# Expert tiles with three buffers in place of two, two PSUM banks for each tile in flight, and a new order of turns, products and results

## What is computed

```python
h = layernorm(x) * (1 + ca) + sa
x = x + ga * mamba(h)                       # conv, selective scan over time, gate, projection
h = layernorm(x) * (1 + cb) + sb
probs = softmax(h @ router_w.T); top_w, top_idx = top_k(probs, 2)
g = einsum('th,eih->tei', h, gate_w)        # E = 8, I = 352, H = 128
u = einsum('th,eih->tei', h, up_w)
y = einsum('tei,ehi,te->th', silu(g) * u, down_w, one_hot_weights(top_w, top_idx))
x = x + gb * y
```

## Time and profile before

| | us |
|---|---|
| median of 3 runs (687.80 to 689.67) | 689.32 |
| the profiled execution | 686.06 |
| its span, first to last instruction | 684.3 |
| TensorE busy | 618.2 (90%) |
| VectorE busy | 552.9 (81%) |
| ScalarE busy | 532.9 (78%) |
| GpSimd busy | 507.5 (74%) |
| scan, up to the first expert tile's load | to about 498 |
| first turn of a tile to the last down product | 500.3 to 669 |
| combination and end | 669 to 684.3 |

### The profile page before, as it was taken

The page is one execution under the profiler, slowest core; times in us unless marked ns, Lnnn a source line. Parts: engine busy times, 40 slices in busy tenths (PEclk is TensorE's granted clock), DMA queues, the critical chain, the costliest instruction groups (busy, mean ns, idle before and its releaser), DMA issues.

```text
span 684.3 us, 14573 instructions
## 1 busy us (share of the span) xinstructions
PE 618.2 (90%) x4473; PEld 518.8 (76%) x4473; DVE 552.9 (81%) x1165; ACT 532.9 (78%) x996; POOL 507.5 (74%) x487
## 2 busy tenths in 40 slices
PE   8988789989989998998998998769789999999995
PEld 6447667867857766786786777658678899999994
DVE  4568797899899999989899999999975586555554
ACT  3689977979998997998999799797834756665650
POOL 5249889877899898899989989977946557644441
PEclk9999999999999999999999999999999999999998
DMA  7303334545634643344544445475612223222545
GB/s 242 125 2 95 95 95 129 157 110 177 208 108 126 172 127 106 117 126 122 158 106 108 107 131 160 118 192 131 176 34 58 65 65 86 82 65 65 154 148 196
DMA packets 65195, 82.93 MB, mean 121 GB/s; under 512 B 6960, under 2 KB 55152, under 8 KB 61024
## 3 DMA queue, kind: packets, MB, share of 16 engines
q1 hardware_dynamic: 59648, 70.78, 38.1%
q0 software_dynamic: 4320, 9.12, 4.0%
q10 hardware_dynamic: 1152, 2.10, 0.8%
HBM read 52.19 MB, written 29.78 MB: 120 GB/s over the span
## 4 chain that ended last, share of the span: by engine, by line
PE 35%; ACT 28%; DVE 14%; issue 11%; POOL 9%; DMA 1%; DVEq 0%; SPq 0%; ACTq 0%; POOLq 0%
PE psum L606 24%; ACT S L1071 10%; PE psum L610 10%; ACT dA L1079 10%; DVE ring L1466 7%; POOL ring L576 5%; POOL S L555 2%; POOL token_rows L477 1%; ACT xn L982 1%; ACT L1019 1%; ACT soft L1010 1%; DMA ring<-results 1%; ACT h2r L1044 1%; ACT soft L1019 1%; ACT soft L1012 1%
## 5 line engine op out<-in xcount | busy, mean ns | idle before, releaser
L576 POOL TENSOR_TENSOR ring<-ring,Cb 128x1024 f32<-128x1024 f32 x128 | 279.2, 2182 | 46.0 <-DVE ring L1466 45.4
L610 PEld LDWEIGHTS psum<-ident,S 128*128 128x128 f32 x1024 | 120.9, 144 | 111.7 <-issue 54.4
L610 PE MATMUL psum<-ident,S 128*128 128x128 f32 x1024 | 161.3, 282 | 41.9 <-POOL S L555 17.3
L1079 ACT ACTIVATE dA<-delta,A 128x512 f32<-128x512 f32 x256 | 178.3, 715 | 10.5 <-DVE ring L1466 10.3
L1071 ACT ACTIVATE S<-duT,BT 128x256 f32<-128x256 f32 x384 | 166.4, 500 | 22.3 <-issue 13.3
L610 PE MATMUL psum<-ident,ring 128*128 128x128 f32 x1088 | 161.3, 280 | 4.0 <-DMA ring<-results 3.7
L1466 DVE TENSOR_TENSOR_SCAN ring<-dA,state,psum 128x512 f32<-128x512 f32 x128 | 157.8, 1266 | 2.5 <-PE psum L610 1.9
L1466 DVE TENSOR_TENSOR_SCAN ring<-dA,psum 128x512 f32<-128x512 f32 x128 | 150.0, 1205 | 2.5 <-PE psum L610 2.2
L610 PEld LDWEIGHTS psum<-ident,ring 128*128 128x128 f32 x1088 | 131.2, 146 | 5.0 <-DMA ring<-results 4.2
L598 POOL DMA_INDIRECT results<-xn,result_at x71 | 68.8, 969 | 74.6 <-DVE xn L1583 64.9
L606 PE MATMUL psum<-uT,S 128*128 128x128 f32 x852 | 107.1, 275 | 1.0 <-DVE uT L1561 1.0
(11 more groups left out here) (218 smaller groups left out, 726.8 us busy)
## 6 DMA issues: line engine op xcount, KB each, us to landing
Cb<-c_rows SPq DMA_DIRECT2D x32, 1024.0 KB, 6.0
token_rows<-zeros SPq DMA_DIRECT2D x64, 272.0 KB, 7.1
uT<-token_rows SPq DMA_DIRECT2D x71, 68.0 KB
ring<-results SPq DMA_DIRECT2D x8, 512.0 KB, 4.9
xT<-in_xT SPq DMA_DIRECT2D x4, 512.0 KB, 5.0
out_T<-xT ACTq DMA_DIRECT2D x8, 256.0 KB, 2.3
stage<-in_xT SPq DMA_DIRECT2D x6, 256.0 KB, 7.1
gateup_w<-in_gate SPq DMA_DIRECT2D x1, 1408.0 KB, 8.3
```

Source lines behind the costliest of these rows:

```text
L576: nc.gpsimd.tensor_tensor(ring[:, k % RING, :, 0:BANK], ring[:, k % RING, :, 1:], Cb[:, group_ % 2, own, :].unsqueeze(1).to_broadcast([P, ...
L610: return nc.tensor.matmul(out, block_in, ident[at, at], is_transpose=True, start=start, stop=True, skip_group_check=True)
L1079: nc.scalar.activation(dA[:, (k * HALVES + a) % DA_SLOTS, :], delta[:, s % 2, a, :], ACT.Exp, scale=A[:, a, n:n + 1]).then_inc(da_ready, 1)
```

## The change

The slots of `xsT`, `both_w`, silu and `innerT` become three (DEEP = 3); silu and `innerT` move into the space of dA, so that `both_w` has S for itself. Each tile in flight now has two PSUM banks: the gate product and the turn share one (2, 3 or 6), and the up and the down product share the other (4, 5 or 1), at different columns. A step's order is new on each engine that computes: TensorE makes gate and up of tile k, turns tile k+2, and makes down of tile k-2; ScalarE makes silu of k ahead of the weights' copy for k+2; VectorE makes inner of k, copies the turn of k+2 and weights the result of k-2. Gate of tiles 0 to 2, up of tiles 0 and 1 and the first three turns stand between the last `add_state` calls of the scan.

```diff
-XS_SLOTS = 4
+XS_SLOTS, DEEP = 4, 3
...
         def PG(k):
-            return bank(2 + k % 2)
+            return bank((2, 3, 6)[k % DEEP])
+        def PX(k):
+            return PG(k if k else DEEP - 1)[:, NIN * P:BANK]
         def PU(k):
-            return bank((4, 1)[k % 2])
+            return bank((4, 5, 1)[k % DEEP])
         def PO(k):
-            return bank((5, 0)[k % 2])[:, 0:P]
+            return PU(k)[:, NIN * P:BANK]
...
+            def turn_row(k):
...
+                wait(pe, silu_ready, k - DEEP + 1)
+                turn(PX(k), xs[:, slot, 0:HID]).then_inc(xt_filled, 1)
...
-            def up_product(k, par):
-                wait(pe, inner_ready, k - 1)
+            def up_product(k):
+                wait(pe, o_read, k - DEEP + 1)
...
-            def tile(k, par, rnd):
...
+            def tile(k):
+                if k == 0:
+                    gate_product(2)
+                if k == 1:
+                    turn_row(3)
+                    down(0)
+                if 2 <= k < TILES:
+                    if k > 2:
+                        gate_product(k)
+                    up_product(k)
+                if 2 <= k < TILES - 2:
+                    turn_row(k + 2)
+                if k >= 3:
+                    down(k - 2)
...
-            gate_product(0, 0)
-            for k in range(STEPS - LAG, STEPS):
-                for a in range(HALVES):
-                    add_state(k, a)
-            up_product(0, 0)
+            gate_product(0)
+            turn_row(1)
+            for a in range(HALVES):
+                add_state(STEPS - 3, a)
+            up_product(0)
+            gate_product(1)
+            for a in range(HALVES):
+                add_state(STEPS - 2, a)
+            up_product(1)
+            turn_row(2)
+            for a in range(HALVES):
+                add_state(STEPS - 1, a)
...
+            def tile(k):
+                if k == 1:
+                    copy_weights(3)
+                if 2 <= k < TILES:
+                    activate(k)
+                if 2 <= k < TILES - 2:
+                    copy_weights(k + 2)
...
+            def tile(k):
+                if 2 <= k < TILES:
+                    inner(k)
+                if 1 <= k < TILES - 2:
+                    turned(k + 2)
+                    result_places(k + 2)
+                if k == 1:
+                    weighted(0)
+                if k >= 3:
+                    weighted(k - 2)
...
             for gap in range(TAIL_GAP):
-                if gap == 3:
-                    turned(0, 0)
-                if gap == TAIL_GAP - 1:
-                    result_places(0)
-                gap_work(gap, SEGS)
+                if gap == 0:
+                    turned(0)
+                if gap == 1:
+                    turned(1)
+                gap_work(gap, SEGS)
+                if gap in (3, 5):
+                    inner((gap - 3) // 2)
+                if gap == 4:
+                    turned(2)
+                if gap == TAIL_GAP - 1:
+                    for k in range(DEEP):
+                        result_places(k)
```

More of the change, by code:

```diff
@@ L201, in adaln_kernel @@
         front_all = uT[:, :, :].rearrange("p c m -> p (c m)")
-        xs, xsT = tiles_of(front_all, 0, XS_SLOTS, ROW), tiles_of(front_all, (XS_SLOTS + 1) * P, 2)
+        xs, xsT = tiles_of(front_all, 0, XS_SLOTS, ROW), tiles_of(front_all, (XS_SLOTS + 1) * P, DEEP)
         ob = tiles_of(xn[0], 0, XS_SLOTS)
         s_all = S[:, :, :, :].rearrange("p r c m -> p (r c m)")
-        silu, innerT = (tiles_of(s_all, 2 * k * NIN * P, 2, NIN * P) for k in range(2))
-        both_w = tiles_of(s_all, 4 * NIN * P, 2, INTER + NIN * P)
+        both_w = tiles_of(s_all, 0, DEEP, INTER + NIN * P)
+        dA_all = dA[:, :, :].rearrange("p r t -> p (r t)")
+        silu, innerT = (tiles_of(dA_all, k * DEEP * NIN * P, DEEP, NIN * P) for k in range(2))
         psum = ctx.enter_context(nc.psum_tensor("psum", [P, 8 * BANK], fp32))
@@ L232, in stat_bank @@
             return bank(f if f < 2 * SEG else 7)
-        PX = bank(6)[:, 0:P]
         def PMX(h):
@@ L323, in tile_schedule @@
             for t in range(TILES + 2):
-                rnd = min(t // XS_SLOTS, (TILES - 1) // XS_SLOTS)
                 if t < TAIL_TILES:
                     beside(2 * t)
-                tile(t, t - rnd * XS_SLOTS, rnd)
+                tile(t)
                 if t < TAIL_TILES:
@@ L882, in beside, with gate_product, down @@
                 gap_work(gap % GAPS, SEGS + gap // GAPS)
-            def gate_product(k, par):
+            def turn_row(k):
+                slot, rnd = k % XS_SLOTS, k // XS_SLOTS
+                if k == FULL_TILES:
+                    pe.wait_ge(group[1], GROUP_STEPS[1])
+                pe.wait_ge(xs_loaded[slot], 16 * (rnd + 1))
+                if k == DEEP - 1:
+                    pe.wait_ge(xt_read, 1)
+                wait(pe, silu_ready, k - DEEP + 1)
+                turn(PX(k), xs[:, slot, 0:HID]).then_inc(xt_filled, 1)
+            def gate_product(k):
                 pe.wait_ge(xt_read, k + 1)
                 pe.wait_ge(weights_copied, k + 1)
-                wait(pe, silu_ready, k - 1)
+                wait(pe, silu_ready, k - DEEP + 1)
                 for c in range(NIN):
-                    last = product(PG(par)[:, c * P:(c + 1) * P], both_w[:, par % 2, c * P:(c + 1) * P], xsT[:, par % 2, :])
+                    last = product(PG(k)[:, c * P:(c + 1) * P], both_w[:, k % DEEP, c * P:(c + 1) * P], xsT[:, k % DEEP, :])
                 last.then_inc(g_filled, 1)
-            def up_product(k, par):
-                wait(pe, inner_ready, k - 1)
-                if k == 1:
+            def up_product(k):
+                wait(pe, o_read, k - DEEP + 1)
+                if k == DEEP - 1:
                     pe.wait_ge(y_out, SEGS)
                 for c in range(NIN):
-                    last = product(PU(par)[:, c * P:(c + 1) * P], both_w[:, par % 2, INTER + c * P:INTER + (c + 1) * P], xsT[:, par % 2, :])
+                    last = product(PU(k)[:, c * P:(c + 1) * P], both_w[:, k % DEEP, INTER + c * P:INTER + (c + 1) * P],
+                                   xsT[:, k % DEEP, :])
                 last.then_inc(u_filled, 1)
-            def down(k, par, e):
+            def down(k):
+                e = pe.value_load(expert[0:1, ds(k, 1)], min_val=0, max_val=EXPERTS - 1)
                 if k == 0:
@@ L904, in down @@
                 pe.wait_ge(inner_ready, k + 1)
-                wait(pe, o_read, k - 1)
-                if k == 1:
-                    pe.wait_ge(read["prefix"], EARLY_SEGS + 1)
                 for c, (i0, w) in enumerate(INNER):
-                    last = product(PO(par), innerT[0:w, par % 2, c * P:(c + 1) * P],
+                    last = product(PO(k), innerT[0:w, k % DEEP, c * P:(c + 1) * P],
                                    down_w[0:w, c, ds(e * HID, HID)], c == 0, c == NIN - 1)
@@ L917, in combine @@
                 if h == 1:
-                    pe.wait_ge(xt_read, TILES)
+                    pe.wait_ge(silu_ready, TILES)
                 wait(pe, mt_read, h - 1)
```

74 lines of the change are left out of this document (28 added, 46 removed).

## The result

The changed kernel took **708.21 us** (median of 4 runs, 705.49 to 709.52), the kernel before 688.56 in the same comparison (4 runs, 686.75 to 689.67): 1.0276 times as long, 95% interval 1.0239 to 1.0313. The prediction was 704.1 us with a range of 691 to 711 and 0.85 on slower. The sign was right, and the time lies 4.1 us above the forecast. The profiled execution is the one of 705.49 us, with a span of 703.0 us at a mean granted clock of 0.985.

What follows compares the result with a forecast made beforehand. It took TensorE, busy 20.00 of 20 us late in the run, as the bound. Terms 7.2 + 7.0 + 0 + 0.6 = 14.8 us on the median 689.32 gave 704.1 us, range 691 to 711.

Steps and rivals of the forecast that it cites:

- The steady steps: Tiles 23 to 70: up waits for weighted through inner and the copy, 0.15 us a step, +7.2 us (5.8 to 8.6).
- the rival: Expert's register load between turn and down comes out by 0.15 us a step, adding 9 us, to 713; chance 0.05.
- The shorter path: Steady steps: loop from up over down and weighted to next up, 2.12 to 2.18 us; alone it would cost 1.4 us.
- The mixed steps: Steps 3 to 22, with the last segment's tail beside: extra waits in shared queues, +7.0 us (3.0 to 8.5).
- Turn of x: Behind step 3: TensorE waits 1.53 us instead of 0.88 for VectorE's addition to x, +0.65 us.
- normalising: Ahead of step 8: inner and weighted stand behind VectorE's wait for GpSimd's root, +1.4 us.
- rows: Turn of rows behind step 9: ScalarE's modulation now stands behind silu and the weights' copy, +1.0 us.
- logits: Behind step 10: wait for ScalarE's copy of the rows, 1.23 us against 0.33, +0.9 us.
- all other steps: Rest of steps 3 to 22: routing and table lumps on VectorE +1.0, the loop's 0.15 in 13 steps +2.0 us.
- The start: First tiles among the ring's last turns: gain of 0.8 us, lost if the lower clock comes; taken as 0 (-0.9 to +0.9).
- The end: Three down products instead of two follow the last up, so the last scatter comes later: +0.6 us (0.3 to 0.9).
- What would show it: Signs: late step 2.24 to 2.30 us, TensorE busy under 20.00 of 20, idle ahead of up, named waits in mixed steps.

Runs made afterwards that it cites:

- own_bank: Changed kernel with the down product of tiles 1 to 70 in a PSUM bank of its own, so up waits only for inner: 696.14 us.
- fixed_down: Changed kernel with down always taking expert 0's weights at a fixed address, so TensorE has no register load before down: 699.74 us.
- sooner_fixed: Changed kernel with weighted ahead of the turn's copy on VectorE and down without its register load: 696.04 us.
- copy_first: Changed kernel with ScalarE copying the weights of tile k+2 ahead of silu of k, as before the change: 704.99 us.
- own_copy_root: Changed kernel with down's own bank, weights' copy ahead of silu, and GpSimd's last normalising root at tile 3 instead of 5: 692.65 us.
- weighted_sooner: Changed kernel with VectorE weighting the result of k-2 right behind inner of k, ahead of the turn's copy: 706.63 us.
- down_first: Changed kernel with down of k-2 at the head of TensorE's step and its weighting ahead of inner of k on VectorE: 700.12 us.
- extra_before: Kernel before the change with one extra 128 x 128 copy on VectorE behind the turn's copy in every tile: 686.88 us.
- before_root: Kernel before the change with GpSimd taking the last normalising root at tile 3 instead of tile 5: 687.82 us.
- unmixed: Changed kernel with the ring's last three pairs of turns as one block between tile 0's gate and tile 1's turn: 712.69 us.
- extra_after: Changed kernel with one extra 128 x 128 copy on VectorE behind the turn's copy in every tile: 709.97 us.
- own_copy: Changed kernel with down in its own bank and ScalarE's weights' copy ahead of silu: 693.70 us.

## Why the prediction was right, and where it failed

- **What bounds the kernel: right.** TensorE had no gap in a late tile, so a deeper ring had nothing to win there; own_bank, the ring without its price, gives 2.12 us a step and no less.
- **The steady steps: the size right (7.2 for 7.9), the mechanism half.** The failed step is "TensorE, not VectorE, gets the gap ... ahead of up", with the loop through inner and the copy as the only one, and the rival's "the load has no wait of its own and can be taken ahead". The loop exists, and fixed_down measures it alone: 2.228 us, just under the forecast's 2.24 to 2.30. The piece from weighted's end through up to the next inner takes 1.08 to 1.09 (1.04 + 0.09 was taken), the others are as in the rows. But alone it would cost 47 x 0.107 = 5.0 us. The register load was priced at nothing with a chance of 0.05; behind a held up product it stands in TensorE's own queue, and that loop is the longer one, 2.29 on average. It adds 2.9 us more (47 x 0.062). It was never the 0.15 on top of the other that the rival had (713 us), since the loops run side by side and the longer one counts. The two errors, 0.04 too long and one loop too few, nearly cancel, so that the size came out in part by luck.
- **The shorter path: right**, 2.12 to 2.18 forecast, 2.16 measured in sooner_fixed. So the rule of the Trainium skill that the prediction set against its rows (Perfetto Trace Analysis, Optimizing Tensor Performance, Matmuls) would have come out at under a quarter of the gap: by this path alone the step grows by 0.04, measured it grew by 0.17. What the prediction left out of this path is the register load, with which it is the longer of the two loops. For separate banks, the rule's own case, the trace agrees: with a bank apart from up's, down's result holds nothing up (own_bank, 2.12).
- **The mixed steps: 7.0 for 8.1.** Turn of x 0.65 forecast, 0.47 measured; normalising 1.4 and 1.47; rows 1.0 and 0.84; logits 0.9 and 0.83; all other steps 3.0 and 2.9, without the lower clock. Their reasons are shown by copy_first (rows and logits) and own_copy_root (the root); that of the turn of x is argued from the order alone. The lower clock behind the logits had no term in the sum: 1.6 us, from its two steps between turns (5.28 + 2.80 us, against 4.28 + 2.16 in weighted_sooner, which waits 1.00 us at the same place and kept the full clock).
- **The start: the term right in this execution (-0.85 in -0.9 to 0.9), its bound for the lower clock too small.** The forecast was that the lower clock would turn the gain into a loss of 0.8. In the profiled executions of weighted_sooner, copy_first and down_first, whose tiles' start is the changed kernel's but for those edits, the granted clock from 498 to 508 us was 0.66 to 0.70, and the first three steps took 12.9 us instead of 10.0: 2.9 more, a loss of about 2.0. But the kernel before is no fixed measure here either: its profiled execution had 0.83 in that window, extra_before 1.00 and before_root 0.66, and from the first turn to gate of tile 3 they took 15.92, 15.64 and 16.73 us. At the full clock on both sides the change gains 0.6 (14.40 and the 0.67, against 15.64); at 0.66 to 0.70 on both sides it loses about 1.3 (17.35 in copy_first and the 0.67, against 16.73). The other three runs of the changed kernel are 1.8 to 4.0 us slower than the profiled one at a lower mean clock (0.972 to 0.977 against 0.985), which fits; their traces weren't taken, so that it is the start isn't shown.
- **The end: 0.6 for 1.3.** The last scatter is 0.77 later, about as worked out. The other 0.5 us, in the last two groups of the combination, had no term; they go with the lower clock there, and aren't shown to be the change's. From the last scatter's start to the end it is 13.93 us before and 14.45 after, but 14.50 in extra_before and 14.80 in before_root, which have the tiles of before.
- **What would show it: two signs failed.** "TensorE busy for less than 20.00 of 20" did not come for its products, with the step at 2.29, but only for its weight loads (19.09). And the idle time did not come ahead of up (0.0 at its products and its loads) but ahead of the weight loads of down (3.1 us from 590 to 660 us), where the register load stands. The rest of the wait is inside the records.
- **The scan.** The first turn came at 500.30 us before and 502.47 after. Over all profiled executions it lies at 499.89 to 501.50 with the tiles of before (3) and at 500.69 to 502.60 with the changed ones (11). These overlap; whether the change moves it by about 1 us is left open.

## What to carry to other kernels

A buffer ring is as deep as its shallowest shared part: three slots with up and down in one bank gave a chain from each tile to the next, and a fourth piece, one spare bank for down, took it away. Before letting an engine wait earlier in its queue, list everything behind that wait up to the result that ends the chain, instructions that the profile doesn't count as busy (register loads) included; an instruction that was free because the engine got to it early is free no longer. And when an edit to a loop changes nothing, look for a second loop of the same length before dropping the first: only both edits together moved it to 2.16.

## What was not expected of the hardware

- Short waits of TensorE don't appear as idle time of its products: with 0.17 us lost in each step of 2.29, the stretch from 600 to 620 us reads 20.00 us busy. The mean of a product's record (275 ns undisturbed, 279 to 292 here), the count of records (169 for 181) and the busy time of the weight loads (19.09 us for 20.00) tell it.
- The register load's cost varies: where it sets the loop, steps lie between 2.25 and 2.42 us; in each run where it doesn't, all of the 47 but at most one lie within 0.03 us of each other.
- A wait of TensorE can cost more than itself through the clock, but need not. The granted clock was 0.50 for some 3.4 us behind the logits' wait of 1.00 us in the changed kernel; the lower level followed a wait at the same place in own_bank, down_first and unmixed, and the wait for the normalised rows in fixed_down and sooner_fixed. With the same waits, weighted_sooner and extra_after kept 1.00 from 520 to 560 us. No kernel without the waits of rows and logits (copy_first, own_copy, own_copy_root and those with the tiles of before) had it there.
- The same lower clock came at the start in some executions and not in others of nearly the same program (granted 0.66 to 1.00 from 498 to 508 us).
